# A macaron transformer block on one core: the weights phase with full-width gate and up, scales in PSUM, rounding on ScalarE, attention weights over ScalarE's queue, stores in the next phase

## The chip, the cores and the metric

The kernel runs on one core of one Trainium2 chip. The metric is the device time of one execution in microseconds. TensorE (PE in the profile) multiplies and transposes, VectorE (DVE), ScalarE (ACT) and GpSimd (POOL) work on tiles in the on-chip memory (SBUF) or in the accumulators (PSUM), and SyncE (SP) issues DMAs. Engines run in parallel and wait for one another by semaphores.

## The reference

One block on x of 4096 tokens by 256, in float32. It has three parts, each after a layer norm: half of an FFN, attention with 16 heads of 16 and an added term, and half of the same FFN again.

```python
def fp4_quant_dequant(x):                      # blocks of 16 along the last dim
    xb = x.reshape(shape[:-1] + (shape[-1] // BLOCK, BLOCK))
    scale = jnp.max(jnp.abs(xb), axis=-1, keepdims=True) / 6.0
    scale = jnp.maximum(scale, jnp.float32(1e-12))
    xn = xb / scale
    idx = jnp.searchsorted(_MID, jnp.abs(xn))
    q = _GRID[idx] * jnp.sign(xn) * scale
...
    gate = fp4_linear(x, w_gate)               # both operands quantized; w_gate, w_up 704 x 256
    y = fp4_linear(x, w_up)
    h = jax.nn.silu(gate) * y
    return fp4_linear(h, w_down)               # w_down 256 x 704
...
    x = x + 0.5 * _L0_ffn_ref(_layernorm(x, axis=-1), ...)
    x = x + _L0_attn_ref(_layernorm(x, axis=-1), ...)
    x = x + 0.5 * _L0_ffn_ref(_layernorm(x, axis=-1), ...)
```

The grid is 0, 0.5, 1, 1.5, 2, 3, 4, 6. The weights don't change between the two FFNs.

## The kernel before, in words

The program is a sequence of phases, each a block in which every engine has its own list of instructions; a phase begins on all engines when the one before has ended on all. They are: the weights phase, the first FFN phase, the projections, attention, the output phase, and the second FFN phase. Attention is a loop of 128 steps (16 heads by 8 blocks of 512 queries).

The weights phase (L181 to L315) prepares all weights. It loads them and x, quantizes gate, up and down by blocks of 16, turns every matrix by TensorE transposes so that the contracted index lies on the partitions, and splits each value in a high part (fp32r, as it is rounded by the copy) and a low part (the remainder), since each product is later made of three (L174 to L178). A "unit" is a piece turned together: its transposes go to one of four PSUM buffers of two banks each (L200, L308), ScalarE's copy gives the high part (L315), VectorE's subtraction the low part (L292). There are 11 units, in the order q, k, v, o, e, gate (two), down (two), up (two) (L232). Unit u waits until the low part of unit u - 4 is made (L305, L306).

Quantizing has a front and a back. The front (L134 to L162) is seven instructions on VectorE: the maximum of each block, the scale, its reciprocal, the reciprocal times ABOVE (a factor just under 1), xn = source times that, the exponent bits of xn (an AND with 0x7F800000, as tensor_scalar), and that power of two bounded from below by 1 and multiplied by 1.5 x 2^22. Adding and subtracting this step rounds xn to the grid; the back (L165 to L171) is that addition, the subtraction and the product with the scale. The backs of gate and up run on GpSimd, that of down on VectorE. Gate and up lie on 88 partitions with 8 x 256 values each, down on 128 partitions with 2 x 768 (704 and padding). All tiles of a front and a back are in SBUF.

VectorE's list is written out by hand: three fronts, the back of down, then the low parts of all units in order, with the statistics of x (bn_stats, L290) ahead of units 5 and 7. TensorE and ScalarE go through the units in order. SP issues gate, up, down, the four attention matrices, We, and x in four chunks; it then waits for all units and issues six stores of the split FFN and output weights to DRAM (L248 to L251), from where the last phases load them again. The phase ends after their issue, not their landing; the first FFN phase waits for them at its own end (L406).

The first FFN phase (L344 on) begins with a chain on VectorE that makes mean and reciprocal root from the statistics (L318 to L336), and then runs 32 tiles of 128 tokens through the quantization, the products and the residual. Its quantization already has the form in which ScalarE makes the rounding step from the power of two by two activations (L548, L550) and VectorE multiplies in one instruction by a reciprocal that lies in PSUM (L494).

Of the kernel before, what the change touches and what calls it, by code (L numbers as in the profile page):

```python
# [30 lines left out]
P = 128  # L31
T = 4096
TT = T // P
D = 256
# [88 lines left out]
class Quant:  # L123


    def __init__(self, src, nb, small, xn, step):
        self.src, self.nb, self.xn, self.step = src, nb, xn, step
        self.amax, self.scale, self.inv = small[:, 0, :], small[:, 1, :], small[:, 2, :]


QUANT_STEPS = 6


def quant_front(dve, quants):  # L134

    for q, chain in quants:  # L140
        chain.settle()
        chain.step(dve.tensor_reduce(q.amax, blocks_of(q.src), AX.X, ALU.max, apply_absolute_value=True))
    for q, chain in quants:
        chain.settle()
        chain.step(dve.tensor_scalar(q.scale, q.amax, 1.0 / 6.0, 1e-12, ALU.mult, ALU.max))
    for q, chain in quants:
        chain.settle()
        chain.step(dve.reciprocal(q.inv, q.scale))
    for q, chain in quants:
        chain.settle()  # L150
        chain.step(dve.tensor_scalar(q.inv, q.inv, ABOVE, None, ALU.mult))
    for q, chain in quants:
        chain.settle()
        chain.step(dve.tensor_tensor(blocks_of(q.xn), blocks_of(q.src), spread(q.inv, q.nb), ALU.mult))
    for q, chain in quants:
        chain.settle()
        chain.step(dve.tensor_scalar(q.step.bitcast(I32), q.xn.bitcast(I32), 0x7F800000, None, ALU.bitwise_and))
    last = []
    for q, chain in quants:
        chain.settle()  # L160
        last.append(dve.tensor_scalar(q.step, q.step, 1.0, 1.5 * 2.0 ** 22, ALU.max, ALU.mult))
    return last  # L162


def quant_back(pool, chain, q, dst, free=None):  # L165

    chain(pool.tensor_tensor(q.xn, q.xn, q.step, ALU.add))
    chain(pool.tensor_tensor(q.xn, q.xn, q.step, ALU.subtract))
    if free is not None:
        pool.wait_ge(*free)  # L170
    return pool.tensor_tensor(blocks_of(dst), blocks_of(q.xn), spread(q.scale, q.nb), ALU.mult)  # L171


# [7 lines left out]
def weights_phase(nc, sem, weights, ident, sel, x_all, x_in, stats, out_w, dram, w_saved):  # L181
# [3 lines left out]
    with ExitStack() as ctx:  # L185
        sb = lambda name, shape, dt=F32: ctx.enter_context(nc.sbuf_tensor(name, shape, dt))
        RP = 88
        RT = I // RP
        raw = [sb("raw_gate", [RP, RT * D]), sb("raw_up", [RP, RT * D]), sb("raw_down", [P, KD * IP])]
        xn = [sb(f"w_xn{n}", [P, RT * D]) for n in range(3)]  # L190
        step = [sb(f"w_step{n}", [P, RT * D]) for n in range(3)]
        raw_attn = [sb(f"raw_attn{n}", [P, KD, D]) for n in range(4)]
        raw_e = sb("raw_e", [DE, D])
        nbm = RT * D // BLK
        small = [sb(f"w_small{n}", [P, 3, nbm]) for n in range(3)]
        quants = []
        for m in range(3):
            rows, nb = raw[m].shape[0], raw[m].shape[1] // BLK
            quants.append(Quant(raw[m][:, :], nb, small[m][0:rows, :, 0:nb], xn[m][0:rows, 0:nb * BLK], step[m][0:rows, 0:nb * BLK]))
        ps = [ctx.enter_context(nc.psum_tensor(f"w_ps{n}", [P, 2, 512], F32)) for n in range(4)]  # L200
# [3 lines left out]
        ident_ready, w_chain, w_front, w_back = sem("ident_ready"), sem("w_chain"), sem("w_front"), sem("w_back")  # L204
        w_turned, w_hi_ready, w_lo_ready = sem("w_turned"), sem("w_hi_ready"), sem("w_lo_ready")
        w_pool, w_dve_back, x_stats = sem("w_pool"), sem("w_dve_back"), sem("x_stats")
# [3 lines left out]
        for m, (hi, lo, at) in enumerate([(out_w["gu_hi"], out_w["gu_lo"], 0), (out_w["gu_hi"], out_w["gu_lo"], I)]):  # L210
            for k in range(KD):
                turns = [(raw[m][:, t * D + k * P:t * D + (k + 1) * P], RP, t // 4, (t % 4) * RP) for t in range(RT)]
                cols = slice(at, at + I)
                units.append((("ffn", m), turns, lambda q: q[:, 0:2, 0:HI],
                              hi[:, k, cols].rearrange("p (a b) -> p a b", a=2), lo[:, k, cols].rearrange("p (a b) -> p a b", a=2)))
        for k in range(0, KI, 4):
            n = min(4, KI - k)
            turns = [(raw[2][:, r * IP + (k + j) * P:r * IP + (k + j + 1) * P], P, j // 2, (j % 2) * D + r * P)
                     for j in range(n) for r in range(KD)]
            units.append((("ffn", 2), turns, lambda q, n=n: q[:, 0:n // 2, :],  # L220
                          out_w["d_hi"][:, k:k + n, :].rearrange("p (a b) c -> p a (b c)", b=2),
                          out_w["d_lo"][:, k:k + n, :].rearrange("p (a b) c -> p a (b c)", b=2)))
        for m, name in enumerate(["q", "k", "v", "o"]):
# [3 lines left out]
        turns = [(raw_e[:, k * P:(k + 1) * P], DE, 0, k * DE) for k in range(KD)]  # L227
        units.append((("attn", 7), turns, lambda q: q[:, 0, 0:KD * DE].rearrange("p (a b) -> p a b", a=KD),
                      out_w["e_hi"][:, :, 0:DE], out_w["e_lo"][:, :, 0:DE]))


        units = units[6:] + units[0:2] + units[4:6] + units[2:4]  # L232

# [1128 lines left out]
```

## Time and profile before

| | us |
|---|---|
| median of 3 runs | 4101.06 (4098.67 to 4104.31) |
| the profiled execution's own time | 4091.76 |
| its span, first to last instruction | 4090.0 |
| TensorE busy | 3806.7 (93%) |
| VectorE busy | 3301.8 (81%) |
| ScalarE busy | 2483.3 (61%) |
| GpSimd busy | 472.8 (12%) |

The span is what lies between the first and the last instruction; the execution's own time has 1.8 us more. The busy times are of the whole span; a phase has other shares. A line number (L292) is the one in the kernel before; where a helper issues an instruction, it is the helper's line. In a timeline "[0.25 <-X]" after a row says how long the engine was idle before it and what released it.

### The profile page before, as it was taken

The numbers are of one execution on the slowest core, as the hardware profiler recorded it, in microseconds if no ns is written. First come the engines' busy times: TensorE is split into PE (matmuls) and PEld (weight loads), VectorE is DVE, ScalarE is ACT, GpSimd is POOL, SyncE is SP. The second block draws the span as 40 slices with busy tenths as digits, with TensorE's granted clock in tenths as the row PEclk, the third lists the DMA queues.
The fourth block names the chain that finished last, engine by engine and source line by source line (L and its number), as shares of the span: only waits on it lengthen the run. The fifth ranks groups of instructions, "written<-read, shape, count | busy, mean of one in ns | idle before, by whom it ended". The sixth has DMA issues, their size and how long they took to land. (4 is left out here: it accounts for less than half of the span.)

```text
span 4090.0 us, 91456 instructions
## 1 busy us (share of the span) xinstructions
PE 3806.7 (93%) x29214; PEld 2212.5 (54%) x29214; DVE 3301.8 (81%) x5171; ACT 2483.3 (61%) x2892; POOL 472.8 (12%) x272
## 2 busy tenths in 40 slices
PE   1997599999999999999999999999999999995698
PEld 1786445555554555555555555555555555553587
DVE  7995488888888888788888888888888888885797
ACT  2663256666666666666666666666666666663464
POOL 3882100000000000000000000000000000000487
PEclk6998799999999999999999999999999999997899
DMA  3002611212122122212121212121212121213200
GB/s 122 1 0 84 160 35 36 44 37 45 36 47 41 41 40 42 44 36 44 36 44 38 44 39 44 38 44 36 44 36 45 38 45 37 47 38 92 69 18 20
DMA packets 316656, 186.52 MB, mean 46 GB/s; under 512 B 195447, under 2 KB 246551, under 8 KB 315831
## 3 DMA queue, kind: packets, MB, share of 16 engines
q1 hardware_dynamic: 316342, 182.35, 20.1%
q8 instruction: 196, 3.21, 0.3%
q14 instruction: 118, 0.96, 0.1%
HBM read 147.75 MB, written 33.82 MB: 44 GB/s over the span
## 5 line engine op out<-in xcount | busy, mean ns | idle before, releaser
L1164 DVE TENSOR_REDUCE tops<-coarse 128x1 f32<-128x512 f32 x4144 | 2681.3, 686 | 578.6 <-PE coarse L1025 475.2
L1140 ACT ACTIVATE probs<-fine 128x1024 f32<-128x1024 f32 x2048 | 1998.5, 1022 | 1014.9 <-PE fine L1044 1014.8
L1055 PE MATMUL o_ps<-probs,vh 128*32 128x512 f32 x8192 | 1088.9, 604 | 0.2 <-ACT probs L1140 0.2
L1034 PE MATMUL fine<-query_a,key_a 64*128 64x512 f32 x4096 | 921.1, 446 | 23.1 <-issue 19.6
L1034 PEld LDWEIGHTS fine<-query_a,key_a 64*128 64x128 f32 x4096 | 386.4, 185 | 929.1 <-ACT probs L1140 750.6
L1025 PE MATMUL coarse<-key_a,max_query 64*128 64x512 f32 x4144 | 832.6, 397 | 43.2 <-DMA key_c<-scratch_c_key 22.3
L1044 PE MATMUL fine<-query_b,key_b 33*128 33x512 f32 x4096 | 816.5, 394 | 0.0
L1040 PE MATMUL fine<-query_c,key_c 64*128 64x512 f32 x4096 | 814.5, 393 | 0.0
L1025 PEld LDWEIGHTS coarse<-key_a,max_query 64*128 64x128 f32 x4144 | 394.2, 186 | 113.5 <-DVE tops L1164 30.0
L1044 PEld LDWEIGHTS fine<-query_b,key_b 33*128 33x128 f32 x4096 | 388.9, 185 | 88.8
L1040 PEld LDWEIGHTS fine<-query_c,key_c 64*128 64x128 f32 x4096 | 389.3, 186 | 82.9
L1055 PEld LDWEIGHTS o_ps<-probs,vh 128*32 128x32 f32 x8192 | 171.7, 108 | 321.1 <-issue 319.5
L890 POOL COPY vh<-v_all 128x512 f32 (+1 forms) x16 | 9.8, 614 | 2840.1 <-PE o_ps L1055 2840.1
L176 PE MATMUL g_ps<-gu_hi,xt_hi 128*128 128x512 f32 (+1 forms) x384 | 153.8, 401 | 37.9 <-DVE xt_lo L448 37.9
L420 POOL TENSOR_TENSOR xn<-xn,step 128x960 f32<-128x960 f32 (+2 forms) x72 | 146.6, 2035 | 80.0 <-ACT step L550 80.0
L421 POOL TENSOR_TENSOR xn<-xn,step 128x960 f32<-128x960 f32 (+2 forms) x72 | 147.1, 2044 | 5.7
L177 PE MATMUL g_ps<-gu_lo,xt_hi 128*128 128x512 f32 (+1 forms) x384 | 146.6, 382 | 0.0
L178 PE MATMUL g_ps<-gu_hi,xt_lo 128*128 128x512 f32 (+1 forms) x384 | 146.5, 382 | 0.0
L176 PE MATMUL y_ps<-d_hi,ht_hi 128*128 128x256 f32 x384 | 116.1, 302 | 15.1 <-DVE ht_lo L459 15.1
L426 POOL TENSOR_TENSOR dst<-xn,scale 128x960 f32<-128x960 f32 (+2 forms) x72 | 127.4, 1769 | 13.4 <-POOL xn L421 11.2
L562 ACT ACTIVATE sg<-g_ps 128x704 f32<-128x704 f32 x64 | 48.6, 759 | 117.4 <-PE g_ps L178 117.4
L178 PE MATMUL y_ps<-d_hi,ht_lo 128*128 128x256 f32 x384 | 111.4, 290 | 0.0
(158 smaller groups left out, 2377.3 us busy)
## 6 DMA issues: line engine op xcount, KB each, us to landing
query_c<-scratch_c_query SPq DMA_DIRECT2D x258, 128.0 KB, 2.6
max_query<-scratch_q_hi SPq DMA_DIRECT2D x524, 32.0 KB, 1.8
max_query<-scratch_c_query SPq DMA_DIRECT2D x262, 64.0 KB, 2.0
query_a<-scratch_q_hi SPq DMA_DIRECT2D x516, 32.0 KB, 1.8
query_a<-scratch_c_query SPq DMA_DIRECT2D x258, 64.0 KB, 2.0
query_b<-neg_max SPq DMA_DIRECT2D x1032, 0.5 KB, 2.0
query_b<-scratch_q_lo SPq DMA_DIRECT2D x258, 32.0 KB, 2.4
scratch_attended<-result SPq DMA_DIRECT2D x512, 8.0 KB
```

Of the source, the lines that this page charges most:

```text
L176: pe.matmul(out, w_hi, m_hi, start=start, stop=False)
L177: pe.matmul(out, w_hi, m_lo, start=False, stop=False)
L178: return pe.matmul(out, w_lo, m_hi, start=False, stop=stop)
L420: chain(pool.tensor_tensor(xn[n][:, cols], xn[n][:, cols], step[n][:, cols], ALU.add))
L421: chain(pool.tensor_tensor(xn[n][:, cols], xn[n][:, cols], step[n][:, cols], ALU.subtract))
L1025: last = pe.matmul(bank[:, :], max_query[n][half_rows(r, 0, HALF), q * P:(q + 1) * P], key_a[keys][half_rows(r, 0, HALF), kb * 512:(kb + 1 ...
L1034: pe.matmul(fine[i % 2][:, r, :], key_a[kp][half_rows(r, 0, HALF), cols], query_a[half][half_rows(r, 0, HALF), :], start=True, stop=False)
L1040: pe.matmul(fine[i % 2][:, r, :], key_c[half_rows(r, 0, HALF), cols], query_c[half][half_rows(r, 0, HALF), :], start=False, stop=False)
L1044: last = pe.matmul(fine[i % 2][:, r, :], key_b[kp][half_rows(r, 0, M_ROW + 1), cols], query_b[half][half_rows(r, 0, M_ROW + 1), :], start= ...
L1055: last = pe.matmul(o_ps[32 * j:32 * (j + 1), :], vh[kp][:, kt, :], probs[:, kt // 2 % RING, kt % 2, :], start=g == 0, stop=g == NG - 1)
L1140: act.activation(probs[:, i % RING, :, :], fine[i % 2][:, :, :], ACT.Exp).then_inc(probs_ready, 1)
L1164: dve.tensor_reduce(tops[n][:, idx // KB, idx % KB:idx % KB + 1], bank[:, :], AX.X, ALU.max).then_inc(tops_ready, 1)
```

## The change

Only the weights phase and the hand-over of its stores are changed.

- Gate and up are 1408 rows together; they are now taken as one list of 11 tiles of 128 rows. The first buffer holds 6 tiles (704 rows of gate, 64 of up), the second 5 (the other 640 rows of up), each tile 256 values a partition. The first is loaded by three DMAs. The columns of the turned result are the same as before.
- The fronts: maxima and reciprocals lie in PSUM, the scales in SBUF for the first two matrices and in PSUM for down. The product takes ABOVE in as a scalar_tensor_tensor. The AND is a tensor_tensor with a constant that lies in one PSUM column. The rounding step is made by ScalarE, in two activations; for down it goes to PSUM.
- There are two PSUM buffers for the units in place of four (unit u waits for the low part of unit u - 2).
- VectorE's order is: front 0, units 0 to 2, front 1, units 3 and 4, front 2, statistics of chunk 0, back of down, units 5 and 6, chunk 1, units 7 and 8, chunks 2 and 3, units 9 and 10. ScalarE's order has the three rounding pairs after units 1, 3 and 4.
- The attention weights are issued on ScalarE's queue, at the head of its list. GpSimd makes ident first.
- SP issues the six stores at the start of the first FFN phase.

```diff
-            quants.append(Quant(raw[m][:, :], nb, small[m][0:rows, :, 0:nb], xn[m][0:rows, 0:nb * BLK], step[m][0:rows, 0:nb * BLK]))
-        ps = [ctx.enter_context(nc.psum_tensor(f"w_ps{n}", [P, 2, 512], F32)) for n in range(4)]
+        ps = [ctx.enter_context(nc.psum_tensor(f"w_ps{n}", [P, 1024], F32)) for n in range(2)]
+        step_ps = ctx.enter_context(nc.psum_tensor("w_step_ps", [P, WIDTH[2]], F32))
+        small_ps = ctx.enter_context(nc.psum_tensor("w_small_ps", [P, 512], F32))
+        inv = [small_ps[:, n * 96:n * 96 + nb] for n, nb in enumerate(NB)]
+        amax = [small_ps[:, 288:288 + nb] for nb in NB]
+        exponent = small_ps[:, 511:512].bitcast(I32)
+        step = [step_sb[0][:, :], step_sb[1][:, :], step_ps[:, :]]
+        scale = [scale_sb[0][:, :], scale_sb[1][:, :], small_ps[:, 384:384 + NB[2]]]
...
-                for m, w in enumerate([wq, wk, wv, wo]):
-                    sp.dma_start(raw_attn[m][:, :, :], w.rearrange("(r p) d -> p r d", p=P)).then_inc(w_loaded[3 + m], 16)
-                sp.dma_start(raw_e[:, :], we).then_inc(w_loaded[7], 16)
...
-                sp.wait_ge(w_hi_ready, len(units))
-                sp.wait_ge(w_lo_ready, len(units))
-                for name in dram:
-                    sp.dma_start(dram[name], out_w[name][:, :, :].bitcast(F32)).then_inc(w_saved, 16)
...
+                    chain(dve.tensor_reduce(amax[m], blocks_of(raw[m][:, :]), AX.X, ALU.max, apply_absolute_value=True))
+                    chain(dve.tensor_scalar(scale[m], amax[m], 1.0 / 6.0, 1e-12, ALU.mult, ALU.max))
+                    chain(dve.reciprocal(inv[m], scale[m]))
+                    chain(dve.scalar_tensor_tensor(out=blocks_of(xn[m][:, :]), in0=spread(inv[m], NB[m]), scalar=ABOVE, in1=blocks_of(raw[m][:, :]),
+                                                   op0=ALU.mult, op1=ALU.mult))
+                    dve.tensor_tensor(step_sb[m][:, :].bitcast(I32), xn[m][:, :].bitcast(I32), exponent.to_broadcast([P, WIDTH[m]]),
+                                      ALU.bitwise_and).then_inc(power_ready, 1)
...
+                front(0)
+                for u in range(0, 3):
+                    split(u)
+                front(1)
+                for u in range(3, 5):
+                    split(u)
+                front(2)
+                statistics(0)
+                dve.wait_ge(step_ready, 3)
+                dve.tensor_tensor(xn[2][:, :], xn[2][:, :], step[2], ALU.add).then_inc(down_chain, 1)
...
+                for m, w in enumerate([wq, wk, wv, wo]):
+                    act.dma_start(raw_attn[m][:, :, :], w.rearrange("(r p) d -> p r d", p=P)).then_inc(w_loaded[3 + m], 16)
+                act.dma_start(raw_e[:, :], we).then_inc(w_loaded[7], 16)
...
+                def rounder(m):
+                    act.wait_ge(power_ready, m + 1)
+                    act.activation(step[m], step_sb[m][:, :], ACT.Relu, scale=MAGIC, bias=around[:, 0:1]).then_inc(above_ready, 1)
+                    act.wait_ge(above_ready, m + 1)
+                    act.activation(step[m], step[m], ACT.Identity, bias=around[:, 1:2]).then_inc(step_ready, 1)
+
+                for u in range(0, 2):
+                    high(u)
+                act.wait_ge(pad_ready, 3)
+                rounder(0)
+                for u in range(2, 4):
+                    high(u)
+                rounder(1)
+                for u in range(4, 5):
+                    high(u)
+                rounder(2)
...
+                    for dst_dram, part in saves[0]:
+                        sp.dma_start(dst_dram, part[:, :, :].bitcast(F32)).then_inc(saves[1], 16)
                     sp.wait_ge(x_done, TT)
-                    sp.wait_ge(*w_saved)
+                    sp.wait_ge(saves[1], 16 * len(saves[0]))
```

## Rows read from the trace of the kernel before

**Rows 1.** Busy time by stretches: bounds, length, each engine's busy, clock, DMA, GB/s

```profile
0.00:80.40 80.40, 10.76 (x62) 9.64 (x62) 65.31 (x67) 8.45 (x13) 27.44 (x21) 0.66 0.40 121
...
610.00:3700.00 3090.00, 3067.66 (x24748) 1608.95 (x24748) 2563.62 (x4085) 2027.76 (x2234) 8.59 (x14) 1.00 0.20 41
```

**Rows 2.** Timeline of the weights phase: start us, duration us, engine, line, tiles

```profile
8.20 2.28 DVE L142 TENSOR_REDUCE w_small<-raw_gate 88x128 f32<-88x2048 f32 x1 [8.20 <-DMA raw_gate<-in_L_ffn_w_gate]
...
10.51 0.22 DVE L145 TENSOR_SCALAR w_small<-w_small 88x128 f32<-88x128 f32 x1
...
26.13 3.67 POOL L171 TENSOR_TENSOR raw_gate<-w_xn,w_small 88x2048 f32<-88x2048 f32 x1
26.17 5.78 DVE L154 TENSOR_TENSOR w_xn<-raw_up,w_small 88x2048 f32<-88x2048 f32 x1
...
39.13 0.75 DVE L148 RECIPROCAL w_small<-w_small 128x96 f32<-128x96 f32 x1
...
49.00 0.96 DVE L157 TENSOR_SCALAR w_step<-w_xn 128x1536 int32<-128x1536 int32 x1
...
58.78 5.31 DVE L290 BATCH_NORM_STATS2 stats<-x_all 128x6 f32<-128x256 f32 x16
...
60.05 2.77 PE L308 MATMUL w_ps<-ident,raw_down 128*128 128x128 f32 x12
...
72.55 1.68 DVE L292 TENSOR_TENSOR gu_lo<-w_ps,gu_hi 128x704 fp32r<-128x704 f32 x2
74.32 0.35 SPq L251 DMA_DIRECT2D saved_gu_hi<-gu_hi  x1
...
78.74 1.25 SPq L251 DMA_DIRECT2D saved_o_lo<-o_lo  x1
...
80.43 0.21 DVE L322 TENSOR_TENSOR mean<-stats 128x32 f32<-128x32 f32 x1 [6.20 <-PEq L234]
```

**Rows 3.** Groups by line, 0 to 80.3 us: busy us, mean ns; last row: one line's min/median/max

```profile
L151 DVE TENSOR_SCALAR w_small<-w_small 88x128 f32<-88x128 f32 (+1 forms) x3 | 7.5, 2507 | 0.1
L145 DVE TENSOR_SCALAR w_small<-w_small 88x128 f32<-88x128 f32 (+1 forms) x3 | 5.7, 1896 | 0.1
L154 DVE TENSOR_TENSOR w_xn<-raw_down,w_small 128x1536 f32<-128x1536 f32 x1 | 5.3, 5265 | 0.0
...
L154 DVE TENSOR_TENSOR w_xn<-raw_gate,w_small 88x2048 f32<-88x2048 f32 x1 | 2.3, 2289 | 0.0
...
L292 DVE TENSOR_TENSOR q_lo<-w_ps,q_hi 128x512 fp32r<-128x512 f32 x1 | 0.7, 683 | 0.0
...
L315 ACT ACTIVATE d_hi<-w_ps x2: 592/808/1024, 62.0 to 62.9; 128x1024 fp32r<-128x1024 f32 x1, 128x512 fp32r<-128x512 f32 x1
```

**Rows 4.** Lines of the first FFN phase: duration ns min/median/max, first and last start

```profile
L494 DVE SCALAR_TENSOR_TENSOR xn<-small_ps,src x36: 424/1134/1159, 85.9 to 332.4; 128x960 f32<-128x960 f32 x28, 128x256 f32<-128x256 f32 x4, 128x704 f32<-128x704 f32 x4
...
L459 DVE TENSOR_TENSOR ht_lo<-ht_ps,ht_hi x32: 956/958/960, 124.1 to 348.7; 128x768 fp32r<-128x768 f32 x32
...
L548 ACT ACTIVATE step<-step,around x36: 492/1096/1099, 87.2 to 333.9; 128x960 f32<-128x960 f32 x28, 128x256 f32<-128x256 f32 x4, 128x704 f32<-128x704 f32 x4
...
L420 POOL TENSOR_TENSOR xn<-xn,step x36: 723/2268/2283, 88.3 to 335.8; 128x960 f32<-128x960 f32 x28, 128x256 f32<-128x256 f32 x4, 128x704 f32<-128x704 f32 x4
...
L426 POOL TENSOR_TENSOR dst<-xn,scale x36: 621/1968/2127, 89.9 to 339.3; 128x960 f32<-128x960 f32 x28, 128x256 f32<-128x256 f32 x4, 128x704 f32<-128x704 f32 x4
```

**Rows 5.** Stretches with DMA traffic: the last two columns are DMA share and GB/s

```profile
2.00:8.00 6.00, 0.00 (x0) 0.00 (x0) 0.00 (x0) 0.03 (x1) 0.89 (x5) 1.00 0.84 184
...
12.00:25.00 13.00, 3.63 (x16) 3.28 (x16) 12.82 (x7) 2.39 (x4) 7.95 (x2) 0.90 1.08 344
...
30.00:74.30 44.30, 7.13 (x46) 6.37 (x46) 43.85 (x56) 4.76 (x7) 12.66 (x3) 0.54 0.00 0
```

**Rows 6.** Timeline of the FFN phase: a VectorE product beside a GpSimd instruction

```profile
135.58 2.13 POOL L426 TENSOR_TENSOR dst<-xn,scale 128x960 f32<-128x960 f32 x1
...
135.95 0.87 DVE L453 TENSOR_TENSOR src<-sg,g_ps 128x704 f32<-128x704 f32 x1
```

More of the change, by code:

```diff
@@ L120, in spread @@
     return ap.unsqueeze(2).to_broadcast([ap.shape[0], nb, BLK])
[L123 to L171, printed above, removed]
 def three_products(pe, out, w_hi, w_lo, m_hi, m_lo, start, stop):
@@ L186, in weights_phase @@
         sb = lambda name, shape, dt=F32: ctx.enter_context(nc.sbuf_tensor(name, shape, dt))
[L187 to L191, printed above, removed]
+        GT, UT = 6, 5
+        WIDTH = [GT * D, UT * D, KD * IP]
+        NB = [width // BLK for width in WIDTH]
+        raw = [sb(f"raw{m}", [P, width]) for m, width in enumerate(WIDTH)]
@@ L192, in weights_phase @@
+        xn = [sb(f"w_xn{m}", [P, width]) for m, width in enumerate(WIDTH)]
+        step_sb = [sb(f"w_step{m}", [P, width]) for m, width in enumerate(WIDTH)]
+        scale_sb = [sb(f"w_scale{m}", [P, nb]) for m, nb in enumerate(NB)]
         raw_attn = [sb(f"raw_attn{n}", [P, KD, D]) for n in range(4)]
         raw_e = sb("raw_e", [DE, D])
[L194 to L198, printed above, removed]
-            quants.append(Quant(raw[m][:, :], nb, small[m][0:rows, :, 0:nb], xn[m][0:rows, 0:nb * BLK], step[m][0:rows, 0:nb * BLK]))
@@ L216, in weights_phase @@
[L216 to L222, printed above, removed]
@@ L274, in _, with split @@
+                    pool.wait_ge(back_chain, 2 * m + 2)
+                    pool.tensor_tensor(blocks_of(raw[m][:, :]), blocks_of(xn[m][:, :]), spread(scale[m], NB[m]), ALU.mult).then_inc(w_back, 1)
             @block.vector
             def _(dve):
-                chain = Chain(dve, w_chain)
-                for m in range(3):
-                    dve.wait_ge(w_loaded[m], 16)
+                chain = Chain(dve, front_chain)
+                chain(dve.memset(exponent, EXPONENT))
+                def split(u):
+                    dve.wait_ge(w_hi_ready, u + 1)
+                    dve.tensor_tensor(units[u][4], turned(u), units[u][3].bitcast(F32), ALU.subtract).then_inc(w_lo_ready, 1)
@@ new lines, in _ @@
+                dve.wait_ge(step_ready, 3)
+                dve.tensor_tensor(xn[2][:, :], xn[2][:, :], step[2], ALU.add).then_inc(down_chain, 1)
+                dve.wait_ge(down_chain, 1)
+                dve.tensor_tensor(xn[2][:, :], xn[2][:, :], step[2], ALU.subtract).then_inc(down_chain, 1)
+                dve.wait_ge(down_chain, 2)
+                dve.tensor_tensor(blocks_of(raw[2][:, :]), blocks_of(xn[2][:, :]), spread(scale[2], NB[2]), ALU.mult).then_inc(down_back, 1)
+                for u in range(5, 7):
+                    split(u)
@@ L293, in _ @@
+                statistics(1)
+                for u in range(7, 9):
+                    split(u)
+                statistics(2)
+                statistics(3)
+                for u in range(9, 11):
+                    split(u)
                 dve.wait_ge(x_stats, TT)
```

117 lines of the change are left out of this document (66 added, 51 removed).

## The prediction

> **What bounds the kernel now.** I read the stages first, because a mean over the span says nothing about a phase that lasts 80 us [rows 1]. The weights phase and what follows it up to the first instruction of the FFN phase take 80.4 us of 4090.0. In it VectorE is busy 65.3 us, TensorE 10.8, ScalarE 8.5 and GpSimd 27.4. Everything from 80.4 on runs code that the change leaves alone but for SP's stores. Next I read VectorE's timeline of that phase [rows 2]. It starts at 8.20, released by the load of gate, has no idle time worth a row, and its last split ends at 72.55 + 1.68 = 74.23. Then SP issues six stores, from 74.32 to 78.74 + 1.25 = 79.99, and the next phase begins at 80.43. So the chain is load (8.2), VectorE (66.0), SP's issues (5.8), phase change (0.44).
>
> Within VectorE's 66.0 us much is no work. The multiplication of raw_up shows 5.78 us; it starts at 26.17, just behind GpSimd's 3.67 us instruction at 26.13 [rows 2]. The same form on raw_gate took 2.29 us [rows 3], so 3.49 was waiting for GpSimd to finish. The one on raw_down shows 5.27, where 2.29 scaled to its 1536 elements is 1.7: again 3.5 [rows 3]. The small tensor_scalars on w_small take 0.22 us when undisturbed [rows 2], and in sum 5.7 and 7.5 us in three each [rows 3]: 5.0 and 6.8 us of waiting. Together VectorE loses 3.5 + 3.5 + 5.0 + 6.8 = 18.8 us behind GpSimd.
>
> **Durations of the new instructions.** Each comes from two widths of the same form [rows 4], drawn to 1536 elements (1280 for the second matrix). The product with a PSUM operand: 424 ns at 256, 1134 at 960, so 1.01 ns an element, 1.72 us (1.46). tensor_tensor with one PSUM operand: 683 at 512 [rows 3], 958 at 768, so 1.78 (1.51). ScalarE's rounding step: 492 at 256, 1096 at 960, so 1.59 (1.37); two are 3.2 (2.8) with gaps. GpSimd's add or subtract: 723 and 2268, so 3.53 (2.97); its product 3.07 (2.6). The maximum, 2.28 at 2048 [rows 2], becomes 1.74 (1.47), the reciprocal of 96 scales 0.75 [rows 2] (0.65), the scale 0.22. A split of 512 columns takes 0.68, of 768 0.96, of 1024 by the same line 1.2; sixteen bn_stats 5.31 [rows 2].
>
> The AND as tensor_tensor of int32 with a broadcast operand in PSUM has no row. The nearest above is 1.78 us; the tensor_scalar that it replaces gives the other end, 0.96 at 1536 [rows 2]. A halved rate would be 3.4. I take 1.78, as its operands lie as those of that row do, and keep 0.96 to 3.4: -2.3 to +4.6 us over three. ScalarE writing to PSUM (once) has no row either; at half or one and a half times its 1.59 it moves the end by -0.7 to +1.6, partly behind bn_stats.
>
> One front is then: 1.74 + 0.22 + 0.75 + 1.72 + 1.78 and four gaps of 0.04 = 6.4 us; for the narrow matrix 5.45. The multiplication by ABOVE (3 x 0.22) goes into the product and the three step multiplications go to ScalarE.
>
> **Do these still wait for GpSimd?** Two rows say no for one PSUM operand [rows 6]: the product src <- sg, g_ps takes 0.87 us at 135.95 with GpSimd's 2.13 us instruction running since 135.58. And the PSUM product never rises over 1.16 us in 36 instances [rows 4]. In the new order every VectorE instruction that can meet GpSimd has at most one SBUF tensor input, or is a maximum, a reciprocal or bn_stats. The Trainium skill (SBUF — State Buffer, "Who interferes with whom") has the rule: two SBUF inputs contend with a GpSimd instruction that reads SBUF, at most one outside the two-port modes does not. By it the 18.8 us go wholly; by rows 6 the same.
>
> **The first load.** Gate landed at 8.20. The load becomes three DMAs of 786 KB together against 721, and ScalarE's queue now sends 1.08 MB beside it, where SP sent that behind it. From 2 to 8 us 184 GB/s were moved, from 12 to 25 us 344, at a mean share near 1 in both [rows 5]. Lower end: nothing competes and the higher rate holds; 786 KB at 344 GB/s from 2.5 and about 1.9 us of latency, 6.7. Upper end: the two queues share evenly; 1.57 MB have to move, and by 8.2 some 1.15 MB had (6 x 184 plus the start); the remaining 0.42 MB, and a skew between the 16 engines of as much again (gate's 0.72 MB were done when 1.15 had moved), take 2.4 to 4.6 us at the two rates: at most some 12. I take 9.5, a little over the middle, 1.3 us later than now. The Trainium skill (DMA: Bandwidth & Descriptors, "Queues, rings and completion order") says that one ring per issuing engine sits on the same 16 DMA engines and that these alternate between rings. That speaks against the new queue and by it the time would lie at the upper end, 2.5 us over my sum; no row of before shows two queues.
>
> **The sum**, in us from the span's start; E0, E1, E2 are the ends of the three fronts.
> - E0 = 9.5 + 6.4 = 15.9. Splits 0 and 1 until E0 + 1.3. ScalarE has done its copies 0 and 1 and rounds until E0 + 3.3; copy 2 (0.6) stands behind the rounding, so split 2 ends at E0 + 4.65. VectorE idles 2.8.
> - Front 1 ends at E1 = E0 + 10.1. Split 3; ScalarE rounds until E1 + 2.85, its copy 4 stands behind it, split 4 ends at E1 + 3.4. VectorE idles 2.5.
> - Front 2 ends at E2 = E1 + 9.8 = E0 + 19.9. Eight bn_stats (2.66) lie beside ScalarE's rounding (3.3); idle 0.65. The three down instructions, 3 x 1.78, end at E2 + 8.75.
> - GpSimd's back of matrix 0 runs from E0 + 3.3 to E0 + 13.5, of matrix 1 to E0 + 22.2. TensorE wants the first for unit 5, whose copy stands behind ScalarE's third rounding at E2 + 3.3 = E0 + 23.2, and the second for unit 9 after E2 + 14. Both are hidden, by 8 us and more.
> - Splits 5 and 6 until E2 + 10.65, bn_stats until 13.3. With two PSUM buffers in place of four, unit 7 (8 transposes of 0.23 [rows 2]: 1.85) starts only at split 5, its copy (1.02 [rows 3]) is ready at 12.75, hidden by 0.5. If not, each later copy costs its own 1 to 2 us. Splits 7 and 8 until 15.1, sixteen bn_stats until 20.4, splits 9 and 10 (640 wide, 0.8 each) until E2 + 22.0.
> - End of VectorE: 15.9 + 19.9 + 22.0 = 57.8.
>
> The x loads are not in the way: the DMA queue is idle from 30 us on now [rows 5], the bytes are the same, and chunks 0, 1 and 3 are wanted at about 36, 46 and 51. SP's stores move into the next phase, where SP issues nothing else; their 5.8 us of issuing leave the path. The 12 us of transfer then lie over the start of the FFN phase, as some 7 us of them do now. Bounds there: 0 to +3 us. The next phase begins at 57.8 + 0.4 = 58.2 against 80.43, a gain of 22.2 us. The profiled execution took 4091.76 us beside its span of 4090.0, so its own time becomes 4069.5. The median of the runs is 4101.06, 9.3 above, and I carry the difference over: **4079 us**.
>
> **Rivals.**
> - *The main case* with its own bounds: first load 6.7 to 12 (-2.8 to +2.5), AND -2.3 to +4.6, stores 0 to +3, ScalarE -0.7 to +1.6, and 2 to 3 us for the runs themselves (4098.67 to 4104.31). 4073 to 4086; chance 0.73.
> - *PSUM operands do not keep VectorE clear of GpSimd* in the long forms. The products and ANDs of fronts 1 and 2 fall into GpSimd's 18 us; four holds of about 3 (the seen ones are 3.5) are 12 us, gain 10: 4091. Against it stand rows 6 and 4. Chance 0.09.
> - *ScalarE's queue is starved.* The attention weights land last, when all the traffic ends: none is left after 30 [rows 5], and I take 28. ScalarE's copies 0 and 1 stand ahead of its rounding, so the chain behind E0 slips by 28.5 - 15.9 = 12.6 us, gain 10: 4091. For it: SP's x loads are queued early now. Against: it takes a queue passed over wholly, where an even share already lands 1.08 MB by 12, and no row shows such a thing. Chance 0.06.
> - *Given back in the attention loop.* This is the rival on the slower side. The loop runs 128 steps in about 3100 us with TensorE busy 3067.7 of 3090.0 [rows 1]. Its code is the same, but it stands elsewhere in the program, behind a phase of other length. If a step lengthened by 0.11 us, 14 us would return and the result be no change; from 0.24 us a step, 30 us, the kernel is slower by 8 us: 4109. For it speaks only that a 1% effect per step is all that is wanted; against it that the loop has nearly no idle time in which a late instruction could be seen. Chance 0.12, a third of it on the slower side.
>
> **How the numbers follow.** A difference of 0.2% (8.2 us) is about what a measurement can tell from none, so faster means below 4092.9. The main case is faster; of the two cases at 4091 two thirds are, the rest no change; the last case is partly each. Faster 0.84, no change 0.12, slower 0.04. The range, 4072 to 4092, holds the main case, most of the cases at 4091 and leaves the last outside.
>
> **What would show it.** VectorE's first maximum starts near 9.5, its last split ends near 58, and SP's first store is issued after that with the FFN phase's first instruction beside it. No VectorE instruction of the phase is over 1.9 us. Two idle stretches of about 2.5 us before splits 2 and 4 are laid to ScalarE. The AND takes 1.78. From the phase's end on, every stage is as long as now. The prediction is wrong if long VectorE instructions reappear beside GpSimd's, if TensorE waits for the attention weights beyond 16, or if the stages after the first lengthen.

## The result and the profile after

The changed kernel takes 4075.9 us in the median of 6 runs (4070.13 to 4078.71), the kernel before 4101.02 us (6 runs, 4091.66 to 4104.52). The ratio is 0.9937 with a 95% interval of 0.9925 to 0.9949: faster by 0.6%, 25.1 us. The forecast was 4079 with 4072 to 4092. The profiled execution took 4071.05 us with a span of 4069.2; that of before had 4091.76 and 4090.0.

The busy time of the first stretch answers [rows 1], the stretch from 2 to 8 us [rows 5]; the columns are those of these groups.

```profile
0.00:55.20 55.20, 11.48 (x52) 9.19 (x52) 41.20 (x62) 16.73 (x19) 20.02 (x23) 0.95 0.43 135
...
2.00:8.00 6.00, 1.78 (x8) 1.41 (x8) 0.18 (x1) 1.88 (x2) 1.01 (x6) 1.00 0.99 291
```

The first stretch is 55.2 us long instead of 80.4. VectorE's busy time in it fell by 24.1 us; 18.8 us of the former time were waits for GpSimd, which count as busy. ScalarE's rose by 8.3, the rounding.

The timeline of the same stretch, changed kernel (start, duration, engine, line, tiles), answers [rows 2]:

```profile
5.44 1.08 PE L300 MATMUL w_ps<-ident,raw_attn 128*128 128x128 f32 x4 [5.44 <-DMA raw_attn<-in_L_attn_Wq]
...
7.82 1.76 DVE L249 TENSOR_REDUCE w_small_ps<-raw 128x96 f32<-128x1536 f32 x1 [6.93 <-DMA raw<-in_L_ffn_w_up]
...
10.71 1.76 DVE L252 SCALAR_TENSOR_TENSOR w_xn<-w_small_ps,raw 128x1536 f32<-128x1536 f32 x1
12.50 1.75 DVE L254 TENSOR_TENSOR w_step<-w_xn,w_small_ps 128x1536 int32<-128x1536 int32 x1
...
15.96 1.57 ACT L317 ACTIVATE w_step<-w_step,w_around 128x1536 f32<-128x1536 f32 x1
17.44 0.58 ACT L311 ACTIVATE v_hi<-w_ps 128x512 fp32r<-128x512 f32 x1
17.68 3.43 POOL L230 TENSOR_TENSOR w_xn<-w_xn,w_step 128x1536 f32<-128x1536 f32 x1 [14.10 <-ACT w_step L317]
...
18.05 0.69 DVE L243 TENSOR_TENSOR v_lo<-w_ps,v_hi 128x512 fp32r<-128x512 f32 x1 [2.60 <-ACT v_hi L311]
...
21.15 1.49 DVE L252 SCALAR_TENSOR_TENSOR w_xn<-w_small_ps,raw 128x1280 f32<-128x1280 f32 x1
21.19 3.43 POOL L232 TENSOR_TENSOR w_xn<-w_xn,w_step 128x1536 f32<-128x1536 f32 x1
22.67 1.49 DVE L254 TENSOR_TENSOR w_step<-w_xn,w_small_ps 128x1280 int32<-128x1280 int32 x1
...
27.09 0.23 DVE L243 TENSOR_TENSOR e_lo<-w_ps,e_hi 128x64 fp32r<-128x64 f32 x1 [2.33 <-ACT e_hi L311]
...
33.70 1.54 ACT L315 ACTIVATE w_step_ps<-w_step,w_around 128x1536 f32<-128x1536 f32 x1 [6.64 <-DVE w_step L254]
...
36.82 1.75 DVE L271 TENSOR_TENSOR w_xn<-w_xn,w_step_ps 128x1536 f32<-128x1536 f32 x1 [0.54 <-ACT w_step_ps L317]
...
53.37 1.54 DVE L243 TENSOR_TENSOR gu_lo<-w_ps,gu_hi 128x640 fp32r<-128x640 f32 x2
55.19 0.35 SPq L420 DMA_DIRECT2D saved_gu_hi<-gu_hi  x1
...
55.23 0.22 DVE L337 TENSOR_TENSOR mean<-stats 128x32 f32<-128x32 f32 x1 [0.32 <-PEq L195]
```

What to see: the two products of fronts 0 and 1 take 1.76 and 1.49 us, the second with GpSimd's 3.43 us instruction running beside it from 21.19 on; the like one, with 2048 values a partition instead of 1280, took 5.78 before [rows 2]. VectorE is idle three times, before unit 2's split (2.60), unit 4's (2.33) and the down instructions (0.54), each released by ScalarE. SP's first store and VectorE's first instruction of the next phase stand side by side.

After the first stretch the two traces differ too. "Attention" is here from the first to the last exponential, each bound by the first and last start of a line:

| stretch, us | before | changed, three traces |
|---|---|---|
| weights phase | 80.4 | 55.2, 55.3, 55.5 |
| first FFN phase | 274.6 | 275.6, 274.8, 276.5 |
| projections | 171.6 | 172.6, 172.2, 172.0 |
| attention | 3193.9 | 3196.1, 3196.6, 3202.8 |
| last exponential to second FFN phase | 93.7 | 94.9, 93.4, 92.2 |
| second FFN phase | 275.8 | 274.8, 275.6, 278.8 |

The phase gained 25.2 us, the span of the first pair of traces only 20.8. The kernel before was traced once, in the second shortest of its six executions (4091.76 us; the six lie between 4091.66 and 4104.52). Which of the two gains is the effect of the change is a question for the repeats below; the medians differ by 25.1.

### The profile page after: what moved, and what is told of

The parts are those of the page before. It is cut to its first block and busy times, and to the rows that moved or that the text cites. A ratio compares the mean times of both kernels' runs of the same rounds, so it can differ in the third digit from the quotient of the medians.

```text
span 4069.2 us, 91443 instructions
## 1 busy us (share of the span) xinstructions
PE 3809.2 (94%) x29204; PEld 2212.9 (54%) x29204; DVE 3278.9 (81%) x5166; ACT 2492.3 (61%) x2898; POOL 466.6 (11%) x274
## 3 DMA queue, kind: packets, MB, share of 16 engines
q10 hardware_dynamic: 1136, 1.08, 0.1%
## 5 line engine op out<-in xcount | busy, mean ns | idle before, releaser
L1071 PEld LDWEIGHTS o_ps<-probs,vh 128*32 128x32 f32 x8192 | 171.6, 108 | 321.5 <-issue 320.4
L126 PE MATMUL y_ps<-d_lo,ht_hi 128*128 128x256 f32 x384 | 111.1, 289 | 0.0
```

The source lines that it names most:

```text
L126: pe.matmul(out, w_hi, m_lo, start=False, stop=False)
L1071: last = pe.matmul(o_ps[32 * j:32 * (j + 1), :], vh[kp][:, kt, :], probs[:, kt // 2 % RING, kt % 2, :], start=g == 0, stop=g == NG - 1)
```

## The experiments

The most telling quantity is the start of the next phase, read to 0.1 us from one trace: the same kernel gave 55.2, 55.3 and 55.5. This scatter is that of the first load: VectorE's first maximum started at 7.82, 7.90 and 8.08 us, and from there to the next phase it was 47.41, 47.42 and 47.41 us. What a part of the change is worth behind the load is therefore read from the first maximum on. Times of whole executions scatter by 10 us and more. Where a kernel was timed only once, its time is given but nothing rests on it.

### The changed kernel again, and where a few us come and go

> The changed kernel once more, as the reference on this chip. My theory: the weights phase is 25.2 us shorter (next phase from 55.2 us instead of 80.4) and what comes after it varies by a few us from one execution to the next whatever the kernel, so the difference of medians is near 25 and the stages after the first are as in the first trace within 1 us, attention within 3. Rival (given back in the loops): attention is again 2.7 us longer than before's, the median difference is nearer 21.

> The changed kernel again, as the reference for the run beside it. The next phase begins at 55.2 or 55.3; attention, from its first to its last exponential, took 3193.9 to 3205.1 us in the traces so far. Theory (it varies from execution to execution of one kernel): it lies anywhere in that range, away from the 3196.1 and 3196.6 of the two traces of this kernel. Rival (each program has its own length there): 3196 within 1 us.

Measured: 4069.34 us (5 runs, 4065.24 to 4072.4) against 4096.41, ratio 0.9937 (0.9923 to 0.9951); then 4072.62 (6 runs, 4063.72 to 4079.63) against 4101.04, ratio 0.9935 (0.9921 to 0.9949). Differences of 27.1 and 28.4 us. The table has their stretches. Attention was 3196.6 and then 3202.8 us, the second outside the 1 us of the second rival. The first rival had half of its case: attention was 2.7 us longer than before's 3193.9 in the first repeat, but the medians were 27.1 apart and not 21. So one kernel varies by 6.7 us there from one execution to another, and by 4 us in the second FFN phase; the 4.4 us by which the first pair of traces fell short of the phase's gain are within that. Nothing is given back that these runs can show: the three differences of medians are 25.1, 27.1 and 28.4, none of them clearly below the phase's gain. The expectation of a difference near 25 was a little low; the intervals (0.5 to 0.8%, 20 to 32 us) hold the phase's 25.2.

### The stores alone, in the kernel before

```diff
 # weights phase
-                sp.wait_ge(w_hi_ready, len(units))
-                sp.wait_ge(w_lo_ready, len(units))
-                for name in dram:
-                    sp.dma_start(dram[name], out_w[name][:, :, :].bitcast(F32)).then_inc(w_saved, 16)
 # first FFN phase
+                    for dst_dram, part in w_saved[0]:
+                        sp.dma_start(dst_dram, part[:, :, :].bitcast(F32)).then_inc(w_saved[1], 16)
```

> The kernel before with one part of the change alone: SP's six stores issued at the start of the first FFN phase. Theory: next phase begins at 74.7 instead of 80.4 and the FFN phase is as long as before (274.6) within 1 us: 5.8 us faster. Rival (the transfers slow the start of the FFN phase): up to 3 us of it come back in that phase.

Measured: 4092.02 us (11 runs) against 4096.41, ratio 0.9991 (0.9982 to 1.0). The next phase begins at 74.5, and that phase takes 273.2 us. Its timeline, SP's queue and VectorE:

```profile
74.41 0.35 SPq L401 DMA_DIRECT2D saved_gu_hi<-gu_hi  x1
...
72.45 1.68 DVE L287 TENSOR_TENSOR gu_lo<-w_ps,gu_hi 128x704 fp32r<-128x704 f32 x2
74.46 0.21 DVE L317 TENSOR_TENSOR mean<-stats 128x32 f32<-128x32 f32 x1 [0.32 <-PEq L234]
```

The stretch is shorter by 5.9 us, and the stores beside the FFN phase's start show no cost there (273.2 against 274.6). The median moved 4.4 us, which agrees with 5.9 but by itself can hardly be told from no change.

### The small tiles back in SBUF, then the same without GpSimd's part

```diff
-        inv = [small_ps[:, n * 96:n * 96 + nb] for n, nb in enumerate(NB)]
-        amax = [small_ps[:, 288:288 + nb] for nb in NB]
+        inv_sb, amax_sb = [[sb(f"w_{name}{m}", [P, nb]) for m, nb in enumerate(NB)] for name in ("inv", "amax")]
+        inv = [a[:, :] for a in inv_sb]
+        amax = [a[:, :] for a in amax_sb]
...
-        scale = [scale_sb[0][:, :], scale_sb[1][:, :], small_ps[:, 384:384 + NB[2]]]
+        scale = [a[:, :] for a in scale_sb]
```

> The changed kernel with the maxima, scales and reciprocals of all three matrices in SBUF, all else as changed. Theory (a PSUM operand keeps VectorE clear of GpSimd): the products of fronts 1 and 2 and the scale instructions have only SBUF tensor inputs and wait for GpSimd's instructions again; long product rows of 3 to 5 us, next phase at 61 to 63 instead of 55.2. Rival (the gain is from the widths and the order, the holds are gone by the order alone): next phase within 1 us of 55.2.

Measured: next phase at 61.2 us (one execution, 4082.51). VectorE's timeline and GpSimd's of this kernel:

```profile
20.23 1.00 DVE L251 TENSOR_SCALAR w_scale<-w_amax 128x80 f32<-128x80 f32 x1
...
21.95 4.06 DVE L253 SCALAR_TENSOR_TENSOR w_xn<-w_inv,raw 128x1280 f32<-128x1280 f32 x1
...
34.18 3.68 DVE L253 SCALAR_TENSOR_TENSOR w_xn<-w_inv,raw 128x1536 f32<-128x1536 f32 x1
...
21.25 3.42 POOL L233 TENSOR_TENSOR w_xn<-w_xn,w_step 128x1536 f32<-128x1536 f32 x1
24.74 3.94 POOL L235 TENSOR_TENSOR raw<-w_xn,w_scale 128x1536 f32<-128x1536 f32 x1
```

The product that started at 21.95 ended at 26.01, 1.34 us after GpSimd's instruction (24.67); undisturbed it takes 1.49, so it had stood still for nearly all of that instruction. The 5.9 us that these tiles are worth (53.3 us from the first maximum on, against 47.4) lie in four instructions: two products (2.6 and 1.9 over) and two scales (0.8 and 0.7 over). GpSimd is held in turn: its product takes 3.94 where it took 2.81.

In the next kernel GpSimd's three instructions a matrix are replaced by a memset of one column that gives the signal, so gate and up stay unquantized:

> The small tiles in SBUF as in the run before it, and GpSimd's backs of gate and up left out (gate and up are not rounded or scaled back). Theory (the waits are for GpSimd's instructions): no VectorE instruction is longer than with the tiles in PSUM, next phase at 54.5 to 55.5. Rival (SBUF operands are slow by themselves, or short of a port within VectorE): the product rows stay above 2 us and the phase stays near the run before it.

Measured: next phase at 55.1 us (one execution, 4073.51). VectorE's timeline of this kernel:

```profile
21.14 1.49 DVE L249 SCALAR_TENSOR_TENSOR w_xn<-w_inv,raw 128x1280 f32<-128x1280 f32 x1
...
30.03 1.76 DVE L249 SCALAR_TENSOR_TENSOR w_xn<-w_inv,raw 128x1536 f32<-128x1536 f32 x1
```

With both inputs in SBUF the product is as fast as with one in PSUM (1.49, 1.76), as long as GpSimd does nothing. That settles who was waited for. It also shows that GpSimd's backs cost the changed kernel next to nothing: from the first maximum on it is 47.2 us without them.

### The AND in its old form

```diff
-                    dve.tensor_tensor(step_sb[m][:, :].bitcast(I32), xn[m][:, :].bitcast(I32), exponent.to_broadcast([P, WIDTH[m]]),
-                                      ALU.bitwise_and).then_inc(power_ready, 1)
+                    dve.tensor_scalar(step_sb[m][:, :].bitcast(I32), xn[m][:, :].bitcast(I32), EXPONENT, None, ALU.bitwise_and).then_inc(power_ready, 1)
```

> The AND as tensor_scalar from SBUF to SBUF, as before, all else as changed. Theory (this form waits for GpSimd but runs at double rate): front 0 ends 0.8 us earlier, ANDs of fronts 1 and 2 wait 1.4 to 2 us for GpSimd; in sum the next phase begins between 55.2 and 56.5. Rival (no wait in this form): 0.96, 0.8 and 0.96 us in place of 1.75, 1.49, 1.75, next phase at 53.0.

Measured: next phase at 55.9 us (one execution, 4074.23). Its timeline, VectorE:

```profile
12.76 0.96 DVE L254 TENSOR_SCALAR w_step<-w_xn 128x1536 int32<-128x1536 int32 x1
...
22.15 2.62 DVE L254 TENSOR_SCALAR w_step<-w_xn 128x1280 int32<-128x1280 int32 x1
...
32.52 1.80 DVE L254 TENSOR_SCALAR w_step<-w_xn 128x1536 int32<-128x1536 int32 x1
```

The faster form saves 0.8 us in front 0, where GpSimd is quiet, loses 1.1 in front 1 (2.62 for 1.49), and comes out even in front 2 (1.80 for 1.75), where it waited 0.8 us and not the 1.4 to 2 expected. Its first load came 0.27 us later than in the changed kernel; from the first maximum on it needs 47.8 us against 47.4, so the form that the change has is worth 0.4 us, not more.

### ScalarE's rounding undone

```diff
+                    dve.tensor_scalar(step[m], step_sb[m][:, :], 1.0, MAGIC, ALU.max, ALU.mult).then_inc(step_ready, 1)
...
-                    act.activation(step[m], step_sb[m][:, :], ACT.Relu, scale=MAGIC, bias=around[:, 0:1]).then_inc(above_ready, 1)
-                    act.wait_ge(above_ready, m + 1)
-                    act.activation(step[m], step[m], ACT.Identity, bias=around[:, 1:2]).then_inc(step_ready, 1)
```

> The rounding step made by VectorE's tensor_scalar (bound and factor in one, as before) in place of ScalarE's two activations, all else as changed. Theory: VectorE gains the idle time before splits 2 and 4 (4.9 us) and pays 1.0 + 0.8 + 1.6 us for the steps and about 1.7 us of waiting for GpSimd at the second; the next phase begins at 55.5 to 56.5. Rival (ScalarE's rounding carries a real part of the gain): 58 or later.

Measured: next phase at 55.5 us (one execution, 4069.94). Its timeline, VectorE:

```profile
14.05 0.96 DVE L256 TENSOR_SCALAR w_step<-w_step 128x1536 f32<-128x1536 f32 x1
...
17.52 0.69 DVE L243 TENSOR_TENSOR v_lo<-w_ps,v_hi 128x512 fp32r<-128x512 f32 x1 [1.30 <-ACT v_hi L312]
...
23.66 2.02 DVE L256 TENSOR_SCALAR w_step<-w_step 128x1280 f32<-128x1280 f32 x1
...
32.79 1.76 DVE L256 TENSOR_SCALAR w_step_ps<-w_step 128x1536 f32<-128x1536 f32 x1
```

VectorE pays 4.7 us for the three steps (1.2 of it a wait for GpSimd) and saves 4.2 of idle time: 2.60 to 1.30, 2.33 and 0.54 to none. In the change's own order, moving the rounding to ScalarE is worth 0.5 us: from the first maximum on it is 47.88 us against the 47.41 and 47.42 of the three traces of the changed kernel. The next phase begins only 0.2 us later because this kernel's first load came 0.23 us early.

### Gate and up on 88 partitions again

```diff
-        GT, UT = 6, 5
-        WIDTH = [GT * D, UT * D, KD * IP]
+        RP, GT = 88, 8
+        WIDTH = [GT * D, GT * D, KD * IP]
+        ROWS = [RP, RP, P]
...
+                sp.dma_start(gate_up, wg.rearrange("(t p) d -> p t d", p=RP)).then_inc(w_loaded[0], 16)
+                sp.dma_start(raw[1][:, :].rearrange("p (t d) -> p t d", d=D), wu.rearrange("(t p) d -> p t d", p=RP)).then_inc(w_loaded[1], 16)
```

> Gate and up on 88 partitions with 2048 values each, as before, all else as changed. Theory: the first maximum starts at 10.1 in place of 7.8, front 0 takes 8.2 us in place of 6.4, front 1 8.2 in place of 5.5, and the waits for ScalarE's rounding grow by 1.0 and 1.4; the next phase begins at 64.0 to 65.0. Rival (the width is worth only the fronts, since the first load is bound by the bytes): 61.5 to 62.5, first maximum near 8.

Measured: next phase at 63.7 us (one execution, 4085.36), 8.4 us later and 0.3 below the expected range; the first maximum starts at 9.57, not 10.1. Its timeline, VectorE:

```profile
9.57 2.29 DVE L249 TENSOR_REDUCE w_small_ps<-raw 88x128 f32<-88x2048 f32 x1 [8.69 <-DMA raw<-in_L_ffn_w_gate]
...
15.54 2.28 DVE L254 TENSOR_TENSOR w_step<-w_xn,w_small_ps 88x2048 int32<-88x2048 int32 x1
...
22.47 0.69 DVE L243 TENSOR_TENSOR v_lo<-w_ps,v_hi 128x512 fp32r<-128x512 f32 x1 [3.45 <-ACT v_hi L311]
...
35.52 0.22 DVE L243 TENSOR_TENSOR e_lo<-w_ps,e_hi 128x64 fp32r<-128x64 f32 x1 [3.61 <-ACT e_hi L311]
...
63.66 0.22 DVE L337 TENSOR_TENSOR mean<-stats 128x32 f32<-128x32 f32 x1 [0.32 <-PEq L198]
```

The width is the largest single part of the gain: 1.75 us in the first load, 1.8 and 2.7 in the two fronts, 0.85 and 1.3 in the two waits for the rounding; these five make 8.4.

### The second queue, in both directions

The changed kernel with the attention weights issued by SP behind down (its diff is shown), and the kernel before with them on ScalarE's queue (the same move the other way):

```diff
+                for m, w in enumerate([wq, wk, wv, wo]):
+                    sp.dma_start(raw_attn[m][:, :, :], w.rearrange("(r p) d -> p r d", p=P)).then_inc(w_loaded[3 + m], 16)
+                sp.dma_start(raw_e[:, :], we).then_inc(w_loaded[7], 16)
                 xv = x_in.rearrange("a (t p) d -> p (a t) d", p=P)
...
-                for m, w in enumerate([wq, wk, wv, wo]):
-                    act.dma_start(raw_attn[m][:, :, :], w.rearrange("(r p) d -> p r d", p=P)).then_inc(w_loaded[3 + m], 16)
-                act.dma_start(raw_e[:, :], we).then_inc(w_loaded[7], 16)
```

> The attention weights issued by SP behind down, ahead of x, as before; all else as changed. Theory of an even share between the two queues: without the second one the first maximum starts earlier than 7.82, at 6.5 to 7.2; the attention weights land by about 12, before split 0 needs them, and the phase ends 0.6 to 1.3 us earlier. Rival (the second queue costs the first load nothing, the higher rate pays for it): first maximum at 7.8 or later, TensorE's first transposes near 12, and the end within 0.3 us or later.

> The kernel before with one part alone: the attention weights on ScalarE's queue. The same two theories: even share, gate then lands later than 8.20, at 10 to 12, and the next phase begins at 82 or later; rival, no cost: first maximum within 0.5 us of 8.20 and the next phase within 0.5 us of 80.4.

Measured: next phase at 55.1 us for the first, 82.3 for the second (one execution each, 4070.32 and 4101.46). Timeline of the first:

```profile
5.95 1.76 DVE L252 TENSOR_REDUCE w_small_ps<-raw 128x96 f32<-128x1536 f32 x1 [5.06 <-DMA raw<-in_L_ffn_w_up]
...
11.80 1.94 PE L303 MATMUL w_ps<-ident,raw_attn 128*128 128x128 f32 x8 [11.80 <-DMA raw_attn<-in_L_attn_Wq]
...
13.56 0.69 DVE L246 TENSOR_TENSOR q_lo<-w_ps,q_hi 128x512 fp32r<-128x512 f32 x1 [1.18 <-ACT q_hi L310]
...
14.28 1.57 ACT L314 ACTIVATE w_step<-w_step,w_around 128x1536 f32<-128x1536 f32 x1
```

and of the second:

```profile
10.07 2.28 DVE L142 TENSOR_REDUCE w_small<-raw_gate 88x128 f32<-88x2048 f32 x1 [10.07 <-DMA raw_gate<-in_L_ffn_w_gate]
```

The second queue delays the first load by 1.87 us in either kernel (5.95 to 7.82, 8.20 to 10.07). That both pairs give the same figure is partly chance: over all traces the first maximum starts at 5.95 and 6.44 with one queue and full width, at 7.59 to 8.09 with two; at 8.10 and 8.20 with one queue and 88 partitions, at 9.57 and 10.07 with two. So the delay is 1.1 to 2.1 us. Up to the first maximum of the changed kernel (7.82 us) SP's queue had moved 0.90 MB and ScalarE's 0.79: a nearly even share.

In the kernel before the delay is all that the queue does: 1.9 us slower. In the changed one the load gains 1.87 when the queue goes, but then Wq lands near 11.8 and its copy, which stands ahead of ScalarE's first rounding, holds both that rounding (14.28 where it was 14.35) and split 0. So my even-share theory had the direction of the load right but its size too small (6.5 to 7.2 expected, 5.95 measured), and it was wrong for the end: 0.6 to 1.3 us were expected, 0.1 to 0.3 came (55.15 beside 55.23, 55.32 and 55.49). TensorE's first transposes at 11.80 and an end within 0.3 us are what the rival had said, though not for its reason, a load that costs nothing.

### A better order, and the order with SP's queue

```diff
                 front(0)
-                for u in range(0, 3):
+                for u in range(0, 2):
                     split(u)
                 front(1)
-                for u in range(3, 5):
+                for u in range(2, 4):
                     split(u)
                 front(2)
+                split(4)
```

> VectorE's order altered: units 2 and 3 after front 1, unit 4 after front 2, so that the copies which stand behind ScalarE's rounding are not waited for. Theory that the two idle stretches before splits 2 and 4 (2.60 and 2.33 us) are on the path: the next phase begins at 50.1 (between 49.8 and 50.6) instead of 55.2, and the time falls by 5 us. Rival (GpSimd's backs or the two PSUM buffers take over as the bound): TensorE waits for the back of matrix 0 or 1 and the phase begins later than 52.

Measured: next phase at 50.0, 5.3 us earlier. 4068.36 us (5 runs, 4063.13 to 4073.36), ratio to before 0.9934 (0.992 to 0.9948). Its timeline, VectorE:

```profile
20.81 0.68 DVE L243 TENSOR_TENSOR v_lo<-w_ps,v_hi 128x512 fp32r<-128x512 f32 x1
...
28.36 0.22 DVE L243 TENSOR_TENSOR e_lo<-w_ps,e_hi 128x64 fp32r<-128x64 f32 x1
...
50.01 0.21 DVE L338 TENSOR_TENSOR mean<-stats 128x32 f32<-128x32 f32 x1 [0.32 <-PEq L195]
```

Both idle stretches are gone. The median is only 1.0 us below the changed kernel's on the same chip, where 5 were expected: in the profiled execution (4073.36 us) attention took 3205.1 us, the longest of all traces. The phase's gain is shown; that of the whole time is not, for this kernel.

The last kernel also has SP issue the attention weights, as in the run above. Its lists of VectorE and ScalarE against the changed kernel's:

```diff
                 front(0)
-                for u in range(0, 3):
-                    split(u)
                 front(1)
-                for u in range(3, 5):
+                for u in range(0, 2):
                     split(u)
                 front(2)
+                for u in range(2, 4):
+                    split(u)
                 statistics(0)
+                split(4)
...
+                act.wait_ge(pad_ready, 3)
+                rounder(0)
                 for u in range(0, 2):
                     high(u)
-                act.wait_ge(pad_ready, 3)
-                rounder(0)
+                rounder(1)
                 for u in range(2, 4):
                     high(u)
-                rounder(1)
-                for u in range(4, 5):
-                    high(u)
                 rounder(2)
-                for u in range(5, 11):
+                for u in range(4, 11):
                     high(u)
```

> Two findings joined: SP issues the attention weights after down (first maximum at 5.95 in place of 7.82), and the lists of VectorE and ScalarE are moved so that nothing waits for those weights or for a rounding: fronts 0 and 1, units 0 and 1, front 2, units 2 and 3, statistics, unit 4, down. Theory: the next phase begins at 47.5 to 48.5, 7 us earlier than in the changed kernel, and the median is 5 to 9 us below its. Rival (GpSimd's backs, which start at 15.5 and end near 34, or the copies of units 5 and 6 bound it): 50 or later.

Measured: 4063.83 us (5 runs, 4058.56 to 4069.28) beside 4072.62 for the changed kernel and 4101.04 for the one before; ratio to before 0.9916 (0.9902 to 0.993). The next phase begins at 48.1. Its timeline:

```profile
6.44 1.76 DVE L252 TENSOR_REDUCE w_small_ps<-raw 128x96 f32<-128x1536 f32 x1 [5.55 <-DMA raw<-in_L_ffn_w_up]
...
12.95 1.28 ACT L315 ACT_TABLE_LOAD   x1 [12.95 <-DVE w_step L257]
...
48.09 0.22 DVE L335 TENSOR_TENSOR mean<-stats 128x32 f32<-128x32 f32 x1 [0.32 <-PEq L195]
```

It beats both kernels: 7.1 us off the phase (55.2 to 48.1) against the changed kernel's first trace, 7.4 against the one beside it, and 8.8 us in the medians. The executions of the two kernels overlap (4058.56 to 4069.28, 4063.72 to 4079.63), so the phase's figure is the firmer one. The rival is out: GpSimd's backs end at 35.7, and VectorE has no idle row after 6.44. The first maximum came at 6.44 where 5.95 was expected. The loading of ScalarE's table stood ahead of the first rounding, but no wait of VectorE came of it.

## Why the prediction was right

The steps as the prediction put them, in us; E0, E1, E2 are the ends of the fronts.

| step | predicted | measured |
|---|---|---|
| first maximum starts | 9.5 | 7.82 |
| front 0 | 6.4 | 6.43 |
| unit 2's split ends after E0 by | 4.65, idle 2.8 | 4.5, idle 2.60 |
| E1 after E0 | 10.1 | 9.9 |
| unit 4's split ends after E1 by | 3.4, idle 2.5 | 3.2, idle 2.33 |
| E2 after E0 | 19.9 | 19.4 |
| down ends after E2 | 8.75 | 8.5 |
| end of VectorE after E2 | 22.0 | 21.25 |
| phase change | 0.4 | 0.3 |
| next phase begins | 58.2 | 55.2 |

- The load was the largest mis-sized term: 1.7 of the 3 us. Nearly even sharing of the two queues, my upper bound, was the mechanism (0.90 and 0.79 MB up to the first maximum), but I built it on the base of the 88-partition load. The full width alone brought gate in by 5.95 (8.20 before), below the 6.7 that I had as the lower end. The DMA rate from 2 to 8 us is 291 GB/s in the changed kernel against 184 before [rows 5]. The second queue is not what raised it: with one queue and full width it is 285, with two queues and 88 partitions 208 in the kernel before and 222 in the changed one. That the rate would follow from the layout I did not see; the slow rows stood in front of me.
- The Trainium skill (DMA: Bandwidth & Descriptors, "Why a DMA increments its semaphore by 16 and not by 1") says that a DMA is split over the largest number of engines, up to 16, that divides both slowest dimensions, which gives 11 for 88 partitions and 16 for 128, and that each engine used ends with one write to the semaphore. The packet records of the traces agree: in the kernel before, 11 packets of 4 bytes start between 6.30 and 7.22 us, ahead of VectorE's start on gate at 8.20, and the twelve loads together have 182 of them (2 x 11 + 10 x 16); the fourteen loads of the full width on one queue have 224 (14 x 16). The number of engines is not the whole of it: the mean DMA share from 2 to 8 us is nearly the same, 0.84 before and 0.89 with the full width on one queue, and from 4 to 8 us a 1 KB packet took 72 ns in the mean before and 54 with the full width. Why the packets took longer was not tried.
- PSUM operands: right, and shown by undoing them (5.9 us) and by taking GpSimd away. The Trainium skill (SBUF — State Buffer, "Who interferes with whom") has it that two SBUF inputs contend with a GpSimd instruction that reads SBUF, and that whichever comes second waits. The traces agree in both directions: a VectorE product took 4.06 us for 1.49, and a GpSimd product 3.94 for 2.81. Of the 18.8 us of waits before, though, only 6.0 come back with the tiles in SBUF. The two waiting multiplications by ABOVE, 6.9 us of the 18.8, no longer exist; how the rest divides between the order, the widths and the tiles was not tried.
- The AND without a row took 1.75, the 1.78 that I chose by the nearest row; ScalarE into PSUM took 1.54 against my 1.59.
- The stores: 5.9 measured alone, 5.8 predicted, and no cost in the next phase, the lower of my bounds.
- The rest of E2 to the end, 0.75 us too much in my sum, came from gaps between instructions that overlap: two 768-wide splits take 1.81 together where I had 1.9, and so on. Another 0.5 lies between E0 and E2, 0.4 of it in the two idle stretches (2.60 and 2.33 where I had 2.8 and 2.5).
- The rivals: the waits of PSUM operands and the starved queue did not occur (Wq landed first of all, at 5.4). What was to be given back in the attention loop does not show: one kernel varies by 6.7 us there, and no difference of medians is clearly below the phase's gain.
- The time: a phase 3.0 us shorter than forecast is what separates 4079 from the measured 4075.9, and 25.1 from a forecast gain of 22. That the profiled execution came within 1.6 us of its own forecast (4071.05 beside 4069.5) is partly luck: the later stages of that trace were 4.4 us longer than before's.

Undone one at a time from the changed kernel, next phase later by: width 8.4, small tiles 5.9, AND 0.4, rounding 0.5 (these two from the first maximum on), queue -0.1 to -0.3; the stores, done alone, 5.9. These make some 21 of 25.2. The other 4 us are not shown part by part. Candidates are parts that were not tried by themselves (the product that takes in ABOVE, 0.7 by [rows 2] without its waits; the units between the fronts) and interplay: with narrower matrices and another order, fewer instructions are left for GpSimd to hold.

## What to carry to other kernels

Put the small operand of a VectorE product in PSUM where GpSimd works beside it; a form at half the rate that doesn't wait can equal the fast one that does. Use all 128 partitions, for the load as for the work. When work moves to another engine's list, look at what stands behind it there: here the rounding on ScalarE was worth 0.5 us as long as VectorE wanted the copies behind it at once, and asking for them later gained 5.3 us more. The later order with the rounding on VectorE was not run.

## What the runs showed of the hardware

- The loading of ScalarE's table (1.28 us) ran ahead of the first activation's wait in 13 of the 14 traces (at 0.75, or near 4 behind the DMA issues). In the last one, where two waits stand before a rounding as the first activation, it ran behind them, from 12.95, and held the rounding until 14.24. VectorE, which bounds the phase, did not wait for it there. What decides the place was not tried; a cheap activation ahead of the waits would be the thing to try.
- Two DMA queues in place of one, with 1.08 MB on the second, delayed the load that is wanted first by 1.87 us in two pairs of traces, and by 1.1 to 2.1 over all of them.
- A load over 128 partitions of 786 KB let VectorE start at 5.95 and 6.44 us, one over 88 partitions of 721 KB at 8.10 and 8.20: 1.7 to 2.25 us earlier with more bytes. The first had 16 completion writes for each DMA, the second 11.
- Up to the first maximum's start one kernel varied from trace to trace (7.82 to 8.08 us); from there to the end of its first phase it took 47.41, 47.42 and 47.41 us.
- The time of the attention loop varied from 3193.6 to 3205.1 us over 14 traces, with the same code in it.
